# The linear branch's scan in the causal stage, cut into two halves of 512 queries

## The reference

```python
qkv = (x @ Wqkv_w + Wqkv_b).reshape(Bb, Ll, 3, Hh, dd)
...
scores = jnp.einsum('bhid,bhjd->bhij', q, k) * scale
attn = jax.nn.softmax(scores + causal_mask, axis=-1)
y_softmax = jnp.einsum('bhij,bhjd->bhid', attn, v)
retention = 1.0 - jax.nn.sigmoid(Lambda_raw)
k_stp = k * scale

def step(state, inp):
    q_t, k_t, v_t = inp
    hebbian = v_t[..., :, None] * k_t[..., None, :]
    state = retention * state + Gamma * hebbian
    y_t = jnp.einsum('bhij,bhj->bhi', W_static + state, q_t)
    return (state, y_t)
...
y = alpha * y_softmax + (1.0 - alpha) * y_stp
return y @ out_w + out_b
```

## Time and profile before

| What | us |
|---|---|
| median of 3 runs (lowest, highest) | 1891.12 (1886.0, 1892.82) |
| the profiled execution | 1901.14 |
| its span, from first to last instruction | 1899.8 |
| PE busy | 1656.2 (87%) |
| DVE busy | 1276.2 (67%) |
| ACT busy | 1114.6 (59%) |
| POOL busy | 695.8 (37%) |
| the 32 scans, first and last start | 1078.4, 1637.6 |

### The profile page before, as it was taken

How to read it: one execution, slowest core, us unless ns; L and a number is a source line. 1 busy time by engine, 2 the same in 40 slices (tenths; PEclk the granted TensorE clock), 3 DMA queues, 4 the chain that set the end, 5 groups by cost and what they waited for, 6 DMA issues and landing times. The chain is left out here.

```text
span 1899.8 us, 45062 instructions
## 1 busy us (share of the span) xinstructions
PE 1656.2 (87%) x19472; PEld 1024.8 (54%) x19472; DVE 1276.2 (67%) x2059; ACT 1114.6 (59%) x1654; POOL 695.8 (37%) x508
## 2 busy tenths in 40 slices
PE   4588888999999999999997778888888888899999
PEld 2355555677677767776775233343343343466665
DVE  4566645667666666666765868877877886755664
ACT  2265567766676667667763366667766767533221
POOL 5212202444244434424443164555554564411100
PEclk7699898999999999999998699999998999999999
DMA  7674100000000000000014236236327323000000
GB/s 171 161 194 121 22 14 2 2 2 2 1 2 2 2 1 2 2 2 1 2 46 115 68 121 168 68 91 162 74 71 182 75 62 75 23 6 12 6 12 12
DMA packets 38748, 102.27 MB, mean 54 GB/s; under 512 B 3944, under 2 KB 12288, under 8 KB 35284
## 3 DMA queue, kind: packets, MB, share of 16 engines
q1 hardware_dynamic: 38548, 99.38, 20.6%
HBM read 67.12 MB, written 31.46 MB: 52 GB/s over the span
## 5 line engine op out<-in xcount | busy, mean ns | idle before, releaser
L1430 DVE TENSOR_REDUCE arena<-ring 128x2 f32<-128x1024 f32 (+2 forms) x320 | 342.1, 1110 | 87.8 <-PE ring L1287 61.9
L1530 ACT ACTIVATE arena<-ring 128x1024 f32<-128x1024 f32 (+1 forms) x320 | 291.2, 937 | 132.4 <-PE ring L1316 89.1
L1337 PE MATMUL accs<-arena 128*9 128x512 f32 (+3 forms) x1536 | 173.9, 526 | 2.7 <-ACT arena L1530 2.6
L1280 PE MATMUL ring<-arena 48*128 48x512 bf16 (+3 forms) x768 | 129.5, 349 | 40.7 <-DVE arena L1430 19.9
L1309 PE MATMUL ring<-arena 51*128 51x512 bf16 (+3 forms) x768 | 125.0, 344 | 45.4 <-DVE arena L1430 25.1
L2469 POOL TENSOR_TENSOR arena<-arena 128x1280 f32<-128x1280 f32 x28 | 65.3, 2332 | 266.6 <-PE accs L2239 235.2
L2453 POOL TENSOR_TENSOR arena<-arena 128x1024 f32<-128x1024 f32 x32 | 76.0, 2376 | 203.3 <-DVE arena L2329 203.3
L2461 POOL TENSOR_TENSOR arena<-arena 128x512 f32<-128x512 f32 x112 | 141.9, 1299 | 11.3 <-DVE arena L2310 11.3
L292 POOL TENSOR_SCALAR xn<-x,moments,rstd 128x128 f32<-128x128 f32 x88 | 70.5, 815 | 192.4 <-DVE rstd L263 174.2
L2736 ACT ACTIVATE arena<-ring 128x512 f32<-128x512 f32 x80 | 47.7, 597 | 147.3 <-PE ring L2591 140.5
L2696 DVE TENSOR_TENSOR arena<-arena,ring 128x512 f32<-128x512 f32 x80 | 55.0, 687 | 87.8 <-PE ring L2593 74.4
(11 more groups left out here) (345 smaller groups left out, 4275.3 us busy)
## 6 DMA issues: line engine op xcount, KB each, us to landing
arena<-whole_k SPq DMA_DIRECT2D x32, 512.0 KB, 4.7
arena<-whole_q SPq DMA_DIRECT2D x32, 512.0 KB, 6.3
arena<-a_scratch_q SPq DMA_DIRECT2D x16, 384.0 KB, 7.3
arena<-a_scratch_k SPq DMA_DIRECT2D x16, 384.0 KB, 8.8
arena<-c_scratch_q SPq DMA_DIRECT2D x14, 384.0 KB, 8.0
arena<-c_scratch_k SPq DMA_DIRECT2D x14, 384.0 KB, 11.5
a_scratch_k<-arena SPq DMA_DIRECT2D x8, 512.0 KB, 4.1
c_scratch_k<-arena SPq DMA_DIRECT2D x8, 512.0 KB, 4.1
```

The costliest lines, as they stand in the source:

```text
L1280: mm = nc.tensor.matmul(o[r], qs[half(r, SCORE), pair, n * P:(n + 1) * P], ks[half(r, SCORE), pair, a:c], start=True, stop=not diag)
L1337: mm = nc.tensor.matmul(acc[ci % 2][32 * h:32 * h + HD + 1, a - c * BANK:BANK], c_values[b % 2][:, j, r * HEADS // 2 + 2 * g + i, :], weig ...
L1430: nc.vector.tensor_reduce(dst, src, AX.X, ALU.max, negate=True).then_inc(c_max_taken.up(item), 1)
L1530: nc.scalar.activation(view(c_probs[wi % 4]), view(ps), ACT.Exp).then_inc(c_weights_made.up(item), 1)
```

## The change

The scan item of each part becomes two items, for tokens 0 to 511 and 512 to 1023, hung on two weighing steps in a row. The second half starts from the last column of the first, and waits for it. The scale waits for the second half and keeps its place, so that for j = 0 and j = 7 it stands in the same step as the second half, directly behind it. The planner counts each half as 1.25.

```diff
                 for j in range(HD):
                     s = at + 6 * j
                     side[s + (j == 0)].append(("kv", b, j))
-                    side[s + 3 + (j == 0)].append(("scan", b, j))
+                    for h in range(HALVES):
+                        side[s + 3 + h + (j == 0)].append(("scan", b, j, h))
                     more = j < HD - 1
                     side[s + 4 + more].append(("scale", b, j))
...
-                     "scan": (0, (("D", 2.3),), 0), "scale": (0, (("A", 1.2),), 0), "A": (0, (("A", 0.6),), 0)}
+                     "scan": (0, (("D", 1.25),), 0), "scale": (0, (("A", 1.2),), 0), "A": (0, (("A", 0.6),), 0)}
...
-                        _, b, j = item
+
+                        _, b, j, h = item
                         sk = c_spread["k"][j % 2]
                         dv.wait_ge(c_kv_made, (b, j))
-                        nc.vector.tensor_tensor_scan(sk[:, :], c_retain[:, j:j + 1].to_broadcast([P, T]), sk[:, :], 0.0,
-                                                     ALU.mult, ALU.add).then_inc(c_state_made.up((b, j)), 1)
+                        if h:
+                            dv.wait_ge(c_state_made, (b, j, h - 1))
+                        cols = sk[:, h * BANK:(h + 1) * BANK]
+                        nc.vector.tensor_tensor_scan(cols, c_retain[:, j:j + 1].to_broadcast([P, BANK]), cols,
+                                                     sk[:, h * BANK - 1:h * BANK] if h else 0.0,
+                                                     ALU.mult, ALU.add).then_inc(c_state_made.up((b, j, h)), 1)
...
-                        ac.wait_ge(c_state_made, (b, j))
+                        ac.wait_ge(c_state_made, (b, j, HALVES - 1))
```

## The result

| | before | with the change |
|---|---|---|
| median (lowest, highest), us | 1891.97 (1886.0, 1893.31) | 1913.79 (1912.21, 1914.44) |
| runs | 4 | 4 |

The ratio is 1.0108, with a 95% interval of 1.0081 to 1.0135: the change makes the kernel slower by 1.1%, 21.8 us. The forecast was 1895, with a range up to 1907.

A forecast was written before the change was run, and what follows sets the result against it. No engine alone was the bound; PE's missing 106 us were hand-overs through three ring buffers. Losses of 8.0 against gains of 3.9 made +4.1 us, added to 1891.12 for a median of 1895, range 1880 to 1907.

The forecast's parts named there:

- slower by over 0.5%: Outcome class for the whole kernel, chance 0.26; within 0.5% had 0.57 and faster by over 0.5% had 0.17.
- The bubble at the scan: Causal stretch: 17 of 32 scans uncovered on the chain; splitting could win half of each, 19 us at most.
- More work on DVE, +1.7, at most 4.9: DVE: 32 more instructions, 0.1 us for each of 17 on the chain, +1.7 us; upper end 4.9, lower nothing.
- Parts 0, 3 and 5, +6.3: Later second half delays ACT's scale by 1.2, 1.4 and up to 1.3 us; losses of 2.7, 2.7 and 0.9 us.
- Part 6, -2.4: "S" moves ahead of the weighing step, so PE's 1.38 us wait goes; gain of 0.8 us in three batches.
- Part 4, -0.6: POOL's cast, held until the scan ends, would end 1 us sooner ahead of "S"; gain of 0.2 us three times.
- parts 1, 2 and 7, -0.9: First row maximum behind a scan comes 1.1 us sooner; gain of 0.3 us in three batches, all in part 1.
- A: Rival, chance 0.17: second halves fill DVE's idle time, half the 19 us won, 1881; waits for L1430 fall 15 or more.
- B: Rival, chance 0.18: ACT's wait for the scan replaces PE's wait for DVE, 16.6 us, 1908; decides past 15 us.
- C: Rival, chance 0.08: the second half runs into a POOL item and waits for all of it, 12.7 us more, 1908.
- my signs: Included scans of 1.15 to 1.22 us, ACT's scan wait 12 or more, no wait over 1 us at part 6.
- The range: Whole kernel: 1880 to 1907 us over all cases; the forecast's own case reached from 1886 to 1901.

The follow-up runs named there:

- old order, split: Scan split as in the change, second half one weighing step later, all other items ordered as in the kernel before; 1905.03 us, ratio 1.0052.
- the order alone: The changed kernel's list of items, but the first half's item does the whole scan and the second's nothing; 1906.09 us, ratio 1.0071.
- the change, earlier: The changed kernel, planner's moves included, with both halves one weighing step earlier in parts 0, 1, 3, 5 and 7; 1899.21 us, ratio 1.0029.
- split, earlier: Split scan, other items ordered as in the kernel before, both halves one weighing step earlier in parts 0, 1, 3, 5 and 7; 1893.22 us, ratio 0.9998.
- moves of groups 2, 3: The kernel before with its whole scan, plus the planner's moves only in weighing steps of groups 2 and 3 (parts 4 to 7); 1912.07 us, ratio 1.0087.
- halves in a row: The kernel before with each scan cut into two halves directly behind each other in the whole scan's place; 1907.06 us, ratio 1.0062.
- quarters: The kernel before with each scan cut into four quarters of 256 in a row in the old place; 1931.3 us, ratio 1.0187.
- split, earlier, moves 0, 1: Split scan, halves one weighing step earlier in parts 0, 1, 3, 5, 7, planner's moves in groups 0 and 1 alone; against before 1887.88 us, ratio 0.9979.

## Why the prediction was wrong

The chance that I gave to "slower by over 0.5%" was 0.26, and it is what came. The step that failed is the planner's moves: the sum has them as one "S" at -2.4 us, and they cost 11 to 14. The cut by itself was mis-sized as well, at 6.5 us where it cost 10.2. The loss comes apart like this, each part measured in the stage and in the medians (each median taken against the kernel before on the same chip):

| part | measured as | stage, us | medians, us |
|---|---|---|---|
| the cut, second half a step late | (old order, split) - before | +10.2 | +11.1 |
| the planner's moves | (the order alone) - before | +13.6 | +12.2 |
| | the change - (old order, split) | +11.2 | +10.7 |
| | (the change, earlier) - (split, earlier) | +12.8 | +6.4 |
| both halves one step later in parts 0, 1, 3, 5 and 7 | (old order, split) - (split, earlier) | +16.2 | +12.0 |
| | the change - (the change, earlier) | +14.6 | +16.3 |
| the halves, a step earlier | (split, earlier) - before | -6.0 | -0.9 |

The cut costs 10.2 us in the old list, and the list another 11.2: together 21.4. The moves cost much the same with or without the cut. The sizes are good to some 5 us, and the small gain of the earlier halves is one of the stage alone: in the medians it can't be told from nothing.

Where the time goes can be read part by part. The 320 exponentials come in the same order in all kernels, ten to a part. Below is by how much the time from the first exponential of a part to the first of the next grew over the kernel before, summed over the four batches, in us. The rows are rounded, and good to one or two us: in the kernel "moves of groups 2, 3", whose list stands as before up to part 3, parts 0 to 3 come out at 0.0, 0.0, 0.8 and 1.7.

| kernel | 0 | 1 | 2 | 3 | 4 | 5 | 6 | 7 | all |
|---|---|---|---|---|---|---|---|---|---|
| old order, split | 4.0 | 0.5 | 1.2 | 4.1 | 0.2 | -0.6 | 0.7 | 0.2 | 10.2 |
| the order alone | 2.8 | -1.7 | -1.0 | 2.2 | 3.8 | 2.9 | 4.0 | 0.6 | 13.6 |
| the change | 7.1 | -0.5 | -2.8 | 4.2 | 0.6 | 5.0 | 3.8 | 4.0 | 21.4 |
| the change, earlier | 2.0 | -6.3 | -4.9 | 4.6 | -1.3 | 5.1 | 4.3 | 3.2 | 6.8 |
| split, earlier | -0.8 | -4.5 | -1.0 | -0.3 | -1.7 | 3.4 | -2.0 | 1.0 | -6.0 |

**The bubble at the scan.** Up to 19 us for the 17 scans on the chain. What is left of it, net of the added instructions, is at most 6.0 us in the stage and 0.9 in the medians, and only where the second half doesn't come later than the whole scan did. In the change nothing of it shows.

**More work on DVE, +1.7, at most 4.9.** The term was mis-sized. The halves were to take 1.15 to 1.22 us. A first half takes 1.21 us and a second 1.27, and DVE is busy for 5.0 us more in the stage, which is over the upper end. I had bounded the scan by the row maximum, two of which cost 154 ns more than one; here it is (2 x 1243 - 2306) = 180 ns on the mean, and 210 against the scans that met nothing (2.49 against 2.28). In a row, where nothing can be put between them, the pair costs 0.25 from start to end and 0.37 us of stage, 11.9 in all; most of this is slower matmuls, as the last section shows. The page of the Trainium skill that I had cited, "VectorE: DVE Perf Modes" (section on the TRN2 errata), has the right direction, and its 60 ns, which I had worked out as an estimate, is a quarter of what a dependent pair shows.

**Parts 0, 3 and 5, +6.3.** In the old list these three parts cost 4.0, 4.1 and -0.6, together 7.5 us, so this term did not break the forecast, but its working holds only in part. At part 0 the delay was right: 1.2 us forecast and 1.22 measured in the second to fourth batch. What failed there is the step by which ACT's 0.33 us of idle time "gives some back": in the old list part 0 takes 1.2 us longer in each of the three batches, the whole delay, where I took 0.9. In parts 3 and 5 of the changed kernel the scale starts 0.97 us later behind the scan's start (1.4 and 1.3 forecast), and ACT's idle time before it grows by 0.72 and 0.42 us. There the delay is swallowed: with the halves a step earlier ACT doesn't wait at those scales at all, and the two parts cost the same, 4.6 and 5.1 against 4.2 and 5.0. What they lose in the change doesn't come from the late scale. In the old list the scale of part 3 starts only 0.25 us later behind the scan, and why part 3 costs 4.1 us there is open.

So ACT's wait for the scan is a poor measure of the loss. The largest single wait for a scan, 4.82 us at part 0 of the first batch (0.81 before), goes with a part that is 0.6 us longer. Part 7 is another such place. I had said that ACT works through a queue there; in the changed trace it finds the queue empty and sits idle, three times for 0.9 us:

```profile
1528.78 1.24 ACT L1549 ACTIVATE arena<-arena,weights_small 128x1024 f32<-128x1024 f32 x1 [0.91 <-DVE arena L1445]
```

But of the 4.0 us that part 7 costs, 3.2 are still there with the halves a step earlier and no such wait.

Putting both halves a step earlier takes 5.1 us off part 0, 5.8 off part 1 and 2.1 off part 2, and next to nothing off parts 3, 5, 6 and 7 (the change against "the change, earlier"). At part 1 ACT hardly waited for the scan in either kernel (0.07 us); what that place gains there is a gain over the kernel before, too.

**PE's clock.** I had no term for it. In the old list PE is busy for 8.6 us more than before with the same matmuls (491.9 against 483.3, at a mean granted clock of 0.92 against 0.93) and idle for only 1.6 more: nearly all of the cut's price there is slower matmuls. In the changed list it is the other way round, 2.0 busy and 19.4 idle. Whether the clock is a cause or goes along, these runs can't tell.

**Part 6, -2.4.** The sign was wrong: part 6 costs 3.8 us in the change. "S" ahead doesn't wait for ACT any more, as I had said; I had taken for granted that "its parts are long there". They come from POOL, behind read, add and "kv", and the maxima are now joined 2.3 us sooner against that chain. PE waits 1.96 instead of 1.38 us. It isn't the late scale: with the halves a step earlier PE still waits 1.75 us there for POOL.

**The moves as a whole.** This is the step that failed and cost most, and but for the -2.4 it isn't even in the sum: I looked at three places of the order and priced one moved item, where 183 of the 337 "M" and "S" stand elsewhere. They cost 11 to 14 us of stage, nearly all of it PE idle time. By the table, 11.3 of the 13.6 us of "the order alone" lie in parts 4 to 7, and of the 11.2 us that the change has over the old list 12.9 lie there, 3.1 at part 0 and -4.9 in parts 1 to 3. In "the order alone" the longest list of waits of PE for row maxima has grown with it, from 75.4 to 87.9 us between 1040 and 1680:

```profile
PEld ring L1310 <- DVE arena L1431: 87.9, 108, 1.7
```

Without the moves the sum would have been 6.5 where 10.2 was measured; with them, 4.1 where it was 21.4.

**Part 4, -0.6, and parts 1, 2 and 7, -0.9.** L1688 is held for half a scan at most: its mean fell from 1012 to 355 ns, and the longest is 1.17 us, under the 1.3 that I had named. PE's waits for row maxima fell by 4.2 us, or by 1.2 over the whole stages. Both are what I said, and both are small. In the old list parts 4 and 1 are 0.2 and 0.5 us longer, so neither gain can be seen.

**The rivals.** A needed those waits to fall by 15: it is out. B, ACT's wait for the scan, was to decide from 15 us, with the exponentials as late as the scale. The wait is 21.1 us, but the second condition is borne out at part 0 alone. Its 1908 was, with C's, the nearest of all I had written, and part of that is luck: it charges parts 3 and 5 with 8.1 us that don't come from the late scale, and has no moves. C did not happen: no half took over 1.28 us in the changed kernel, and the place where the whole scan met L1649 is free of it. In the kernel with the halves in a row it did happen, at 1266.12 above, and in "split, earlier", so it depends on where the halves fall. The rule of the page "SBUF — State Buffer" of the Trainium skill agrees with both. Of my signs, the waits before "S" at part 6 went the wrong way, and outside the causal stage only the layers ahead of it differ, by 9 us, which the change doesn't touch.

**The range.** Its upper end is too low by its own working. With 4.9 for the instructions, 3.6, 4.2 and 3.9 for parts 0, 3 and 5, and nothing given back, the terms add up to 16.6 us, which is 1908 and not the 1901 that I wrote. The measured time is above that, too.

## What to carry to other kernels

When an operation is cut and the second piece goes to the next slot, look first at who waits for its end: if a waiter stands directly behind it, try the first piece a slot earlier instead of the second a slot later. Here that took back 14.6 of 21.4 us, though it made nothing faster than the whole operation. And if a list comes from a planner that reads the costs that were changed, compare the whole list before and after and hold it fixed in one experiment; here the moves cost as much as the cut itself. And neither the length of a wait nor an engine's idle share says what a delay costs: of two delays of about 1 us in the same ring one was passed on whole and the other swallowed. Compare the same item's start in both kernels further down the list.

## What the runs showed of the hardware

- A scan of 1024 or 512 elements that starts from zero takes 2.28 or 1.21 us in the undisturbed case, so 2.08 ns for an element and 0.15 us for the instruction itself. The quarters of 256, most of which start from a column, take 0.75 (median; mean 0.78). A second half, which takes its starting value from a column of SBUF, takes 61 ns longer than the first, which starts from zero.
- The second of two dependent scans starts 35 ns after the first's end (32 pairs in the kernel with the halves in a row), while an independent DVE instruction starts about 80 ns before it (1453.89 + 2.28 against 1456.08 in the earlier trace rows).
- PE's busy time for the same 5590 matmuls in the stage goes from 478.7 us at a mean granted clock of 0.94 ("split, earlier, moves 0, 1") to 506.1 at 0.89 (quarters). In the kernel with the halves in a row it makes nearly all of the loss: PE is busy for 10.9 us more and idle for 1.0 more, of 11.9. Whether the low clock is there the cause of the loss or goes with it, no run can tell: I know of no edit that changes the clock alone.
